# First attention of a hybrid block: a loop over fourteen sequences, written out on every engine

## The reference

```python
def attn_a(x, Wq, Wk, Wv, Wo):           # x is the normalised input, (16, 512, 256)
    q, k, v = (split_heads(x @ W.T) for W in (Wq, Wk, Wv))   # 16 heads of 16
    scores = jnp.einsum('bhqd,bhkd->bhqk', q, k) * hd ** -0.5
    scores = jnp.where(head_mask[None], scores, neg_inf)     # 8 heads strided, 8 fixed
    attn = jax.nn.softmax(scores, axis=-1)
    out = jnp.einsum('bhqk,bhkd->bhqd', attn, v)
    return out @ Wo.T                     # and x = x + this
```

## Time and profile before

| | |
|---|---|
| median of 3 runs | 3898.58 us (3898.19 to 3899.9) |
| the profiled execution's own time | 3880.78 us |
| its span, first to last instruction | 3879.0 us |
| mean granted TensorE clock | 0.912 |
| first attention in the span | from about 1.8 to about 1180 us |
| bodies 0 to 15 of it | from 47.6 us |
| clock at 0.50 in slot 13 | in bodies 0, 2 and 6, from 97.9, 237.8 and 528.0 us, 6.8 us each |
| clock at 1.00 throughout | from 104.7 to 176.4 us (body 1) and from 1118.5 us to the end of the stage (body 15) |

### The profile page before, as it was taken

One profiled execution on the slowest core, in us unless ns is written; L12 is line 12 of the kernel. 1 busy time (PEld: TensorE's weight loads), 2 busy tenths in 40 slices (PEclk: granted clock), 3 DMA queues, 4 the chain that ended last, 5 costly groups with the idle time before them and its releaser, 6 DMA issues. The chain is left out here.

```text
span 3879.0 us, 79453 instructions
## 1 busy us (share of the span) xinstructions
PE 3193.4 (82%) x24024; PEld 2457.4 (63%) x24024; DVE 2826.8 (73%) x7319; ACT 2134.8 (55%) x5224; POOL 1102.8 (28%) x626
## 2 busy tenths in 40 slices
PE   6888888888892798888488888888888884799898
PEld 4666666666661788887255665556555553688787
DVE  4666666666666788886177878877878873788897
ACT  4666666666671233332177777777777773233333
POOL 1000000000000454553222443334433442455444
PEclk9999899899896899999588999999999986899999
DMA  4244244243331000001145343444344441011100
GB/s 84 41 63 56 41 63 56 41 66 52 48 45 61 6 16 16 16 16 34 48 59 71 54 69 56 70 65 65 59 66 63 62 72 64 23 32 32 32 22 27
DMA packets 133989, 187.60 MB, mean 48 GB/s; under 512 B 15127, under 2 KB 81559, under 8 KB 133143
## 3 DMA queue, kind: packets, MB, share of 16 engines
q1 hardware_dynamic: 133830, 185.95, 28.8%
HBM read 45.65 MB, written 28.84 MB: 19 GB/s over the span
## 5 line engine op out<-in xcount | busy, mean ns | idle before, releaser
L408 ACT ACTIVATE a_probs<-a_probs,a_negmax 128x176 f32<-128x176 f32 (+4 forms) x1024 | 504.6, 493 | 384.9 <-DVE a_negmax L331 384.8
L331 DVE CUSTOM_DVE_ANT_0 a_probs<-a_mask,a_score 128x176 f32<-128x176 f32 (+4 forms) x1024 | 403.5, 399 | 261.5 <-PE a_turned L493 125.6
L493 PE MATMUL a_turned<-ident,a_probs 128*128 128x128 f32 (+1 forms) x2176 | 437.8, 294 | 124.5 <-DVE a_pT L340 115.5
L1075 PE MATMUL f_y_bank<-f_wdT,f_hqT 128*128 128x256 f32 x1536 | 392.7, 410 | 79.1 <-ACT f_hqT L1013 79.1
L1751 ACT ACTIVATE b_u<-b_u,b_negmax 128x512 f32<-128x512 f32 x512 | 367.6, 719 | 98.7 <-DVE b_negmax L1631 98.4
L1631 DVE CUSTOM_DVE_ANT_0 b_u<-b_u,b_score 128x512 f32<-128x512 f32 x512 | 339.9, 681 | 97.7 <-PE b_score L1877 95.7
L1075 PEld LDWEIGHTS f_y_bank<-f_wdT,f_hqT 128*128 128x128 f32 x1536 | 309.3, 206 | 131.0 <-issue 80.4
L1886 PE MATMUL b_turned<-ident,b_u 128*128 128x128 f32 x2048 | 334.7, 290 | 69.7 <-DVE b_pT L1637 39.6
L1623 DVE SCALAR_TENSOR_TENSOR b_u<-b_u,b_score 128x1024 f32<-128x1024 f32 x256 | 309.5, 1215 | 89.8 <-ACT b_u L1744 87.9
L493 PEld LDWEIGHTS a_turned<-ident,a_probs 128*128 128x128 f32 (+1 forms) x2176 | 243.2, 138 | 185.6 <-DVE a_pT L340 122.6
L1886 PEld LDWEIGHTS b_turned<-ident,b_u 128*128 128x128 f32 x2048 | 247.9, 147 | 161.6 <-issue 80.3
(11 more groups left out here) (231 smaller groups left out, 7300.2 us busy)
## 6 DMA issues: line engine op xcount, KB each, us to landing
b_stack<-b_part SPq DMA_DIRECT2D x192, 256.0 KB, 8.2
a_stack_q<-a_part SPq DMA_DIRECT2D x192, 128.0 KB, 4.4
a_stack_k<-a_part SPq DMA_DIRECT2D x192, 128.0 KB, 6.0
xs<-in_x_dram SPq DMA_DIRECT2D x16, 512.0 KB, 8.8
x_before_b<-xs SPq DMA_DIRECT2D x16, 512.0 KB, 2.9
b_xin<-x_before_b SPq DMA_DIRECT2D x16, 512.0 KB, 11.6
b_xres<-x_before_b SPq DMA_DIRECT2D x16, 512.0 KB, 3.8
x_after_b<-b_xres SPq DMA_DIRECT2D x16, 512.0 KB, 3.0
```

The lines of the kernel that those rows point to most:

```text
L331: dve.tensor_tensor_reduce(out=probs[:, n % 2, j, 0:keys(n)], in0=mask_of(n), in1=score[j][:, 0:keys(n)], scale=-1.0, scalar=3.0e38, op0=A ...
L408: act.activation(probs[:, n % 2, j, 0:keys(n)], probs[:, n % 2, j, 0:keys(n)], ACT.Exp, bias=negmax[:, n, j:j + 1], scale=-1.0, accum_out= ...
L493: m = nc.tensor.transpose(turned[j % 2][0:rows, u, :], chunk(n, probs[:, n % 2, j, :], u), ident[:])
L1075: m = mm(y_bank[:, 0:H], hqT[:, t % 2, c * P:(c + 1) * P], wdT[:, c, :], start=c == 0, stop=c == IC - 1)
```

## The change

The three loops of the first attention become loops of the program that writes the instructions: every engine's stream holds each body in full, with s a constant. The waits, the semaphores, the order of the work, the tiles and the DMAs are the same; register arithmetic and the branches back go. Fourteen copies of the middle body stand in the streams of TensorE, VectorE and ScalarE in place of one.

```diff
@@ bodies
     body(0, "first")
-    with engine.Fori(1, SEQS - 1) as s:
+    for s in range(1, SEQS - 1):
         body(s, "middle")
     body(SEQS - 1, "last")
@@ block.sync
-            with sp.Fori(1, SEQS - 2) as s:
+            for s in range(1, SEQS - 2):
                 load(s + 2)
                 place_rest(s)
                 place_all(s)
@@ block.gpsimd
             rstd_of(0)
-            with pool.Fori(1, SEQS) as s:
+            for s in range(1, SEQS):
                 rstd_of(s)
```

## The result

The changed kernel takes 3989.41 us (median of 4 runs, 3985.97 to 3992.05), the kernel before 3898.51 us beside it: ratio 1.0232, 95% interval 1.0214 to 1.025, slower. The profiled executions stand at 3986.6 and 3879.0 us of span, 107.6 us apart where the medians are 90.9 apart: the profiled execution of the kernel before was some 18 us shorter than its other runs.

What follows compares the result with a forecast made beforehand. No engine is saturated; they hand work round a ring, and VectorE's code fetch at branches back lies on the path that sets the end. 72.1 + 7.4 - 19.5 = 60.0 us off 3898.6 gave 3838.6 us, range 3815 to 3874 us.

Steps and rivals of the forecast that it cites:

- The branches back: First attention, VectorE: removing 13 branches back, with their code-fetch gaps, saves 72.1 us, or 5.5 us a body.
- Registers and constants at 0: First attention, all engines: constants in place of register arithmetic gain 0, give or take 4 us.
- More code for TensorE at 0: First attention: TensorE reads some 5 or 6 more code packets a body at cost 0; upper bound 148 us.
- the forecast sign of 0.5 us: TensorE: no issue wait over 0.5 us beside queue 8's about 110 packets; otherwise rival D.
- The clock: First attention, TensorE: falls to 1.2 GHz in 5 of 13 bodies cost 19.5 us; present falls return 7.4 us.
- The stages behind keep their lengths but for the clock: Stages after the first attention: no change in length except through the clock.
- Rival D: First attention: TensorE waits for its own code, 1.90 us a packet; 88 us slower, 3987 us; chance 0.05.

Runs made afterwards that it cites:

- the increments: Throwaway semaphore increments on VectorE ahead of the second attention's loop: 64 in the changed kernel, 3829.48 us; 28 in the kernel before, 4051.69 us.

## Why the prediction was wrong

**The branches back: right.** The gaps of the earlier trace rows were VectorE fetching code that it no longer held, and they went. Forecast 5.5 us a body; VectorE alone written out gives the gain, all the others written out give none, and 7 branches fewer with registers kept give 5.2 us each.

**Registers and constants at 0: right** for the other engines, by the version in which all but VectorE's loop has constants (0.9992). VectorE's own registers were not tried alone; the 5.2 us a branch with them kept leave little of the 5.5 to them.

**More code for TensorE at 0: right.** Queue 8 rose from 43 to 106 packets, forecast about 110, at no cost that can be measured: with TensorE's loop kept the time is 3985 us, with it written out 3989. No matmul of the first attention waits on issue. The weight loads at L493 do, 96.7 us in all against 33.3 before, 1.9 us at the longest against 1.5, over the forecast sign of 0.5 us, but the time does not show it.

**The clock: right in the thirteen bodies, not in the whole stage.** Thirteen bodies at 66.1 us without falls (the shortest now takes 66.0) are 859.3 us; the trace has 878.1, so the falls cost 18.8 us where I had put 19.5. They came otherwise than I had drawn them: whole falls in slot 13 in four bodies, others elsewhere. A fall of 20.5 us in body 15, which I had not priced, stands in the rest of the stage, which gave 6.0 us back; that it is the main part of them is not shown. The whole stage gained 52.6 us, forecast 60.0. That the sum comes so close in the bodies is in part luck: in the other profiled executions with VectorE's first loop written out, GpSimd's first operation of the next stage, at 1128.95 us here, starts anywhere from 1117.74 to 1135.83 us.

**The failed step** is one sentence near the end, "The stages behind keep their lengths but for the clock", and with it the whole part on what more code does. There I asked only who reads the new code. I did not ask what the code does to the place of the code behind it. The second attention's loop on VectorE, 302 instructions, was moved from 12.40 to 41.62 packets, into the stretch where it touches a fourth packet, and a loop that had been read once was then read anew in each of 12 passes, behind the placements. (That it is the place is shown by the increments; the fourth packet is the reading R.) That term was missing from the sum: 12 x 13.5 = 162 us, against 60.0 us forecast as gain and 52.6 measured. In the profiled executions the stretches give -58.6 + 6.0 - 1.4 + 162.8 - 0.9 = 107.9 us; less the 0.3 us by which the first stretch begins earlier, these are the 107.6 us between them.

**Rival D's number,** 3987 us, is the measured time within 3 us, and its cause is wrong. It had TensorE waiting for its own code in the first attention; no matmul there waits on issue, the stage grew shorter, and with VectorE alone written out, where queue 8 stays at 43 packets, the time is the same 3985. The agreement is chance.

The Trainium skill ("Runtime: NRT & Kernel Launch", section on the preamble and postamble breakdown) has instruction fetch prefetching by itself. For straight code the runs agree (0.2 us of issue gap at most on VectorE in the first attention). At a branch back they show that it is not enough: a first gap of 2.8 to 11.4 us where code is fetched anew, and none that the waits show at the second attention's branch in the kernel before, where none is.

The row that could have warned me stood in the trace of the kernel before: one code packet in 12 passes of the second attention's loop, against six in each pass of the first's (78 in 13). It says that this loop is held, that holding may be what makes its branch cheap (0.05 us at 2452 us), and so that it can be lost.

## What to carry to other kernels

When an edit changes the amount of code ahead of a loop, look at every later loop on each engine: how many code packets its passes fetch before, and how many it would touch at its new place. Test a suspicion with a few dozen instructions that do nothing, in the kernel before as well; it costs one run and tells place from work. And a gain read from one stage should be claimed for one engine at a time: here VectorE's loops alone, written out in both attentions, give 3826 us with less new code than the change adds.

## What was unexpected in the hardware

- A loop on VectorE that no longer fits is not a little slower, it is read anew in every pass: 60 packets in 12 passes against 1. 302 instructions fit or don't by where they stand. The first attention's loop, 393 instructions or 3.07 packets, touches at least four wherever it stands and has its gaps in all three versions that keep it; that three packets are held is inferred from this and from the table, not measured by itself.
- TensorE's first loop of 1326 instructions ran from its second pass on with no packet on queue 8: six packets in the first pass, 16 KB each, then none, so it holds far more code than VectorE. ScalarE's first loop of 287 instructions shows no issue gap; why was not tried.
- Code waits in line with data. A missing packet costs 4.05 us with no copy on the DMA engines, 3.6 us behind copies of about 2.0 us, and 11.3 us behind copies of 9.6 us.
- A wait of 11.3 us on another engine also comes with TensorE's clock at 1.2 GHz for 20.4 us. A pass is 2.2 us longer than the gap explains.
- The kernel before, unchanged, ran from 3877 to 3906 us in these comparisons; what makes up that spread was not tracked down.
